# Cross-attention in a decoder layer: packed score operands laid out together in DRAM, read in fewer and earlier DMAs

## The reference, cut to what matters

```python
def _L0_xattn_ref(x, ctx, pos_map, ctx_pos_map, Wq, Wkv, Wout, bout):   # 32 heads of 16
    q = (x @ Wq).reshape(b, n, N_HEADS, HEAD_DIM)
    k, v = jnp.split(ctx @ Wkv, 2, axis=-1)
    ...
    q = apply_axial_rope(q, pos_map)
    k = apply_axial_rope(k, ctx_pos_map)
    logits = jnp.einsum('bqhd,bkhd->bhqk', q, k) * scale
    w = jax.nn.softmax(logits, axis=-1)
    attn = jnp.einsum('bhqk,bkhd->bqhd', w, v)
    return attn.reshape(b, n, N_HEADS * HEAD_DIM) @ Wout + bout
```

## Time and profile before

| what | us |
|---|---|
| median of 3 runs | 1645.27 (1644.57 to 1647.97) |
| the profiled execution, time | 1629.16 |
| the profiled execution, span | 1627.3 |
| TensorE busy in the span | 1380.9 (85%) |
| VectorE busy | 887.9 (55%) |
| GpSimd busy | 504.4 (31%) |
| ScalarE busy | 472.2 (29%) |
| DMA of the hardware queue, share of 16 engines | 21.3% |

### The profile page before, as it was taken

How to read it: one execution, slowest core, us unless ns; L and a number is a source line. 1 busy time by engine, 2 the same in 40 slices (tenths; PEclk the granted TensorE clock), 3 DMA queues, 4 the chain that set the end, 5 groups by cost and what they waited for, 6 DMA issues and landing times. The chain is left out here.

```text
span 1627.3 us, 24455 instructions
## 1 busy us (share of the span) xinstructions
PE 1380.9 (85%) x8442; PEld 1109.1 (68%) x8442; DVE 887.9 (55%) x1532; ACT 472.2 (29%) x731; POOL 504.4 (31%) x348
## 2 busy tenths in 40 slices
PE   5899999945478888888868569999999999999991
PEld 4677777735356566656645458888887879999990
DVE  5666666655556666766643666655556542222225
ACT  3222222223145455444544221111111113332220
POOL 1122222212533233322300230633315056456234
PEclk9999999977679899899988689999999999999996
DMA  6000000003333333333320950324000033345247
GB/s 278 1 1 0 0 0 0 1 1 124 93 109 112 99 93 112 106 99 100 107 67 2 365 207 20 110 85 146 20 20 33 13 130 136 136 139 184 79 125 250
DMA packets 86268, 150.41 MB, mean 92 GB/s; under 512 B 11696, under 2 KB 54832, under 8 KB 83888
## 3 DMA queue, kind: packets, MB, share of 16 engines
q1 hardware_dynamic: 79920, 114.77, 21.3%
q0 software_dynamic: 6272, 34.61, 6.0%
HBM read 88.25 MB, written 60.56 MB: 91 GB/s over the span
## 5 line engine op out<-in xcount | busy, mean ns | idle before, releaser
L972 DVE TENSOR_REDUCE b_mx<-b_rt 128x4 f32<-128x1024 f32 x128 | 156.5, 1223 | 144.1 <-PE b_rt L797 144.1
L1580 DVE SCALAR_TENSOR_TENSOR residual<-c_yp,c_shared,residual 128x512 f32<-128x512 f32 x176 | 127.4, 745 | 143.0 <-PE c_yp L43 142.9
L1114 ACT ACTIVATE b_pf<-b_rt,b_zero 128x1024 f32<-128x1024 f32 x128 | 142.8, 1116 | 215.3 <-PE b_rt L809 214.7
L797 PE MATMUL b_rt<-b_kT,b_qT 64*128 64x256 f32 x512 | 73.9, 371 | 95.6 <-DMA b_qT<-b_low 89.7
L41 PE MATMUL c_fc<-c_xh,c_w 128*128 128x512 f32 x352 | 137.1, 390 | 0.0
L43 PE MATMUL c_fc<-c_xh,c_w 128*128 128x512 f32 x352 | 137.0, 389 | 0.0
L42 PE MATMUL c_fc<-c_xl,c_w 128*128 128x512 f32 x352 | 137.0, 389 | 0.0
L797 PEld LDWEIGHTS b_rt<-b_kT,b_qT 64*128 64x128 f32 x512 | 44.7, 215 | 132.8 <-issue 63.0
L41 PE MATMUL c_fc<-c_ring,c_xTl 128*128 x312 | 105.2, 337 | 0.0
L43 PE MATMUL c_fc<-c_ring,c_xTh 128*128 x312 | 100.6, 322 | 0.0
L42 PE MATMUL c_fc<-c_ring,c_xTh 128*128 x312 | 100.2, 321 | 0.0
(11 more groups left out here) (288 smaller groups left out, 3510.0 us busy)
## 6 DMA issues: line engine op xcount, KB each, us to landing
c_eraw<-in_c_we POOLq DMA_DIRECT2D x8, 2176.0 KB, 9.7
c_xe<-c_rows_in SPq DMA_DIRECT2D x39, 256.0 KB, 3.1
c_rows_out<-c_ye SPq DMA_DIRECT2D x39, 256.0 KB, 2.1
c_rows_in<-c_xe SPq DMA_DIRECT2D x19, 512.0 KB, 10.2
c_rows_out<-c_xe SPq DMA_DIRECT2D x19, 512.0 KB, 10.1
c_wraw<-in_c_ws SPq DMA_DIRECT2D x11, 768.0 KB, 4.3
b_high<-b_hi SPq DMA_DIRECT2D x32, 256.0 KB, 2.3
b_low<-b_lo SPq DMA_DIRECT2D x32, 256.0 KB, 2.3
```

The costliest lines, as they stand in the source:

```text
L797: last = nc.tensor.matmul(rt[:, e, t * S:(t + 1) * S], qT[r, p, t * P:(t + 1) * P], kT[r, p, :], start=True, stop=True)
L972: nc.vector.tensor_reduce(out=mx[:, :, 2 * p:2 * p + 2].rearrange("p t e -> p e t"), in_=rt[:, 0:2, :].rearrange("p e (t s) -> p e t s", s ...
L1114: nc.scalar.activation(pf[:, s:s + 2, :], rt[:, 2:4, :], ACT.Exp, scale=XD ** -0.5, bias=zero[:, :]).then_inc(e_done, 1)
L1580: nc.vector.scalar_tensor_tensor(out=X[:, t, :], in0=yp[:, (n * 4 + k) % 3, :], scalar=shared[:, t:t + 1], in1=X[:, t, :], op0=ALU.mult, o ...
```

## The change

The two DRAM tables become one, `b_pack`, in which the three terms of a head stand below each other in packed order (48 rows, 50 with the two rows of zeros). `rotated_out` now writes `hi` twice, to terms 0 and 2 for k and to terms 0 and 1 for q, and `lo` once. `chunk` has lost its argument e: one call issues four reads, for each e one of 48 rows into `kT` and one of 50 rows into `qT`. Its step is 4f - 4 instead of 4f - 3 and 4f - 2. The semaphore counts follow: `hi_out` gets 64 a group for each c, `chunk_in` 64 instead of 192.

```diff
-    high_dram = nc.dram_tensor("b_high", (B, 2, XD, HP, 2, S), FP32).ap()
-    low_dram = nc.dram_tensor("b_low", (B, 2, XD + 2, HP, 2, S), FP32).ap()
+    pack_dram = nc.dram_tensor("b_pack", (B, 2, 3 * XD + 2, HP, 2, S), FP32).ap()
...
             def rotated_out(g, n):
                 which, c = n // 2, n % 2
-                for k, (table, split, done, out) in enumerate(((high_dram, hi, rh_done, hi_out), (low_dram, lo, rl_done, lo_out))):
+                for split, done, out, terms in ((hi, rh_done, hi_out, ((0, 2), (0, 1))[which]), (lo, rl_done, lo_out, ((1,), (2,))[which])):
                     sp.wait_ge(done, g * 4 + (n + 1))
                     sp.sem_inc(ready, 1)
-                    sp.dma_start(table[g, which, 0:XD, :, c, :].rearrange("(r i) h s -> (i h) r s", r=2),
-                                 as_f32(split[:, :, c, :])).then_inc(out[c], 16)
-
-            def chunk(g, f, e):
+                    for x in terms:
+                        sp.dma_start(pack_dram[g, which, x * XD:(x + 1) * XD, :, c, :].rearrange("(r i) h s -> (i h) r s", r=2),
+                                     as_f32(split[:, :, c, :])).then_inc(out[c], 16)
+
+            def chunk(g, f):
                 c = f // 2
-                if f % 2 == 0 and e == 0:
-                    sp.wait_ge(hi_out[c], g * 32 + 32)
+                if f % 2 == 0:
+                    sp.wait_ge(hi_out[c], g * 64 + 64)
...
-                at = slice(f % 2 * 8 + e, f % 2 * 8 + 8, 2)
-                for which, packed, terms in ((0, kT, (high_dram, low_dram, high_dram)), (1, qT, (high_dram, high_dram, low_dram))):
-                    for x, term in enumerate(terms):
-                        n = XD + 2 if which == 1 and x == 2 else XD
-                        row = 64 * e + 16 * x
-                        sp.dma_start(as_f32(packed[row:row + n, 4 * f:4 * f + 4, :]), term[g, which, 0:n, at, c, :])\
+                for e in range(2):
+                    at = slice(f % 2 * 8 + e, f % 2 * 8 + 8, 2)
+                    for which, packed, n in ((0, kT, 3 * XD), (1, qT, 3 * XD + 2)):
+                        sp.dma_start(as_f32(packed[64 * e:64 * e + n, 4 * f:4 * f + 4, :]), pack_dram[g, which, 0:n, at, c, :])\
                             .then_inc(chunk_in[f], 16)
...
                     for f in range(4):
-                        for e in range(2):
-                            for d in due(i, live, 4 * f - 3 + e):
-                                chunk(b + d, f, e)
+                        for d in due(i, live, 4 * f - 4):
+                            chunk(b + d, f)
...
-                    pe.wait_ge(chunk_in[p // 4], g * 192 + 192)
+                    pe.wait_ge(chunk_in[p // 4], g * 64 + 64)
...
-                    act.wait_ge(hi_out[n % 2], g * 32 + (16 if n >= 2 else 0))
+                    act.wait_ge(hi_out[n % 2], g * 64 + (32 if n >= 2 else 0))
```

More of the change, by code:

```diff
@@ L724, in _ @@
             for g in range(B):
-                sp.dma_start(low_dram[g, 1, XD:XD + 2, :, :, :].rearrange("r h c s -> (r h c) s"),
+                sp.dma_start(pack_dram[g, 1, 3 * XD:3 * XD + 2, :, :, :].rearrange("r h c s -> (r h c) s"),
                              nm[0:64, :, :].rearrange("p t s -> p (t s)")).then_inc(lo_out[g % 2], 16)
@@ L746, in chunk @@
                     sp.sem_inc(ready, 1)
[L747 to L751, removed]
-                at = slice(f % 2 * 8 + e, f % 2 * 8 + 8, 2)
-                for which, packed, terms in ((0, kT, (high_dram, low_dram, high_dram)), (1, qT, (high_dram, high_dram, low_dram))):
-                    for x, term in enumerate(terms):
-                        n = XD + 2 if which == 1 and x == 2 else XD
-                        row = 64 * e + 16 * x
-                        sp.dma_start(as_f32(packed[row:row + n, 4 * f:4 * f + 4, :]), term[g, which, 0:n, at, c, :])\
+                if fresh(g):
+                    sp.wait_ge(presets, 8)
+                else:
+                    sp.wait_ge(st_mm, (g - 1) * HP + (4 * f + 4))
+                for e in range(2):
+                    at = slice(f % 2 * 8 + e, f % 2 * 8 + 8, 2)
+                    for which, packed, n in ((0, kT, 3 * XD), (1, qT, 3 * XD + 2)):
+                        sp.dma_start(as_f32(packed[64 * e:64 * e + n, 4 * f:4 * f + 4, :]), pack_dram[g, which, 0:n, at, c, :])\
                             .then_inc(chunk_in[f], 16)
```

## The result

| | before | changed | |
|---|---|---|---|
| median, us | 1646.62 | 1543.09 | ratio 0.9364, 95% interval 0.9339 to 0.9389 |
| lowest to highest | 1644.57 to 1651.03 | 1539.67 to 1543.8 | 4 runs each |
| span of the profiled execution | 1627.3 | 1541.6 | |

The changed kernel is 103.5 us faster by the medians. The forecast was 1548 (1533 to 1590). I read its trace by the views used before.

A forecast was written before the change was run, and what follows sets the result against it. TensorE was taken to bound cross-attention, waiting for loads queued behind the maxima and slowed by its clock. 74.8 + 4.7 + 24 + 3 - 7 - 2 = 97.5 us off 1645.3 gave 1548 us, range 1533 to 1590.

The forecast's parts named there:

- Chunk waits: Cross-attention score steps: TensorE's 30 waits for the packed operand load go to nothing, gain 74.8 us.
- Clock in the interior: Six interior groups: without the waits TensorE's granted clock holds the full level, gain 6 x 4.0 = 24 us.
- Clock in groups 0 and 7: First and last group: clock gain taken as 3 us for both, their steps being short and bound by VectorE as well.
- VectorE: Late next in the score steps: costs 1.2 us per interior group, 7 us for six, plus 2 us in groups 0 and 7.
- Start and landing: First chunk of cross-attention: usable 2.4 us after its last read's issue, at 426.2 instead of 430.93, gain 4.7 us.
- below 10 us: Sign in the changed kernel's profile: TensorE's wait for `b_pack` below 10 us in all.
- Writes and uneven reads: Doubled high writes cost taken as 0, upper end 8 us; 50-row reads land in 3 to 4 us, hidden by matmuls.
- Clock stays: Rival: TensorE keeps short pauses and its clock still falls, losing 24 + 3 us; time 1575, chance 0.14.
- it does nothing: Rival: the chunk's real releaser is the exponent matmuls of the group before, so no gain; chance 0.01.
- Maxima become late: Rival: maxima stand behind a chunk and writes in SyncE's queue, 32 pay 1 us each; time 1580, chance 0.09.
- Slower: Rival: the 50-row reads run on one engine, a chunk takes 19 us or more; 1808 at the upper bound, chance 0.04.
- Half the wait stays: Rival: packed reads land late because SyncE issues them later than thought; time 1548 + 40 = 1588, chance 0.06.

The follow-up runs named there:

- early12: Kernel before with the new request order alone (chunk at step 4f - 4), keeping its twelve reads and two tables: 1557.5 us, ratio 0.9459.
- filled: Kernel before with 16 idle 256-column matmuls on TensorE ahead of each chunk wait, in every group but the first: 1638.01 us, ratio 0.9962.
- half_max: Changed kernel with the row maximum taken over the first half of the keys only: 1530.67 us, ratio 0.9302.
- packed_late: Changed kernel with its four packed reads requested at the old places, two at step 4f - 3 and two at 4f - 2: 1609.37 us, ratio 0.9781.
- more_writes: Changed kernel with two more writes of the high part per rotated piece, to a DRAM table nobody reads: 1545.29 us, ratio 0.9390.
- split48: Changed kernel with each 50-row read into qT cut into 48 and 2 rows: 1541.38 us, ratio 0.9374.
- b_again: Kernel before, unchanged, run again for a second trace: 1649.48 us, span 1647.7.
- first two sets: Eight follow-up kernels run on one chip beside the kernel before, whose median there was 1644.19 and 1646.25 us.
- the third: Set of three variants of the changed kernel's start, run on another chip beside the kernel before, whose median there was 1624.12 us.

## Why the prediction was right, and where its terms were off

| term | predicted, us | measured, us | from |
|---|---|---|---|
| interior: chunk waits less VectorE | 52.8 - 7 = 45.8 | 48.3 | idle 53.4 to 5.1 |
| interior: clock | 24 | 25.7 | busy 281.6 to 255.9 |
| groups 0 and 7: idle | 22 - 2 = 20 | 17.5 | idle 14.2 to 5.0 and 24.3 to 16.0 |
| groups 0 and 7: clock | 3 | 12.6 | busy 35.8 to 32.7 and 61.0 to 51.5 |
| start | 4.7 | 1.5 | first step 430.93 to 429.45 |
| sum | 97.5 | 105.7 | 103.5 by the medians |

**Chunk waits** (74.8 us, of them 22.0 in groups 0 and 7): right, all 30 are gone, at the margins worked out. `early12` shows that it is the place in the queue that does most of it.

**Clock in the interior** (24 us): right. 25.7 by the traces, and 27.3 by `filled`, where the order and the reads are those of the kernel before and TensorE's pauses are filled.

**Clock in groups 0 and 7** (3 us): mis-sized, 12.6 measured. I charged these groups little because VectorE binds their short steps. In group 7 that didn't hold: its granted clock went from 0.85 to 0.97 and its work from 61.0 to 51.5 us. The 0.83 in the earlier trace rows called for the same reckoning as in the interior. The idle time there fell by 17.5 us instead of 20, since VectorE's waits in the two groups grew by 4.2 us (from 5.1 to 9.4), where I had taken 2.

**VectorE** (1.2 us a group): too dear. Its waits are 4.4 us in the six interior groups, 0.7 a group, and `half_max` puts the whole at 0.8. The 0.41 us wait at step 5 that I read the earlier trace rows was nearly all of it (0.48 now); the 0.9 that I took for it was the middle of a range whose upper end added the DMA wait that had covered it, and the low parts in front of step 13 cost next to nothing.

**Start and landing** (4.7 us): mis-sized, 1.5 measured, and the one term that was wrong in kind. I took 2.4 us from the last read's issue to its use from interior chunks of twelve reads, and kept it for four. Four reads need 5.3 there, 4.9 in `packed_late`, also above the 3 to 4 us that I had allowed for the uneven read. That took 2.9 us back; the first chunk was issued and the low write landed 0.8 us quicker than counted, so from the low write to the first score step it was 8.9 us instead of 6.9. It is also why the wait for `b_pack` came to 12.2 us; the sign "below 10 us" did not fit my own term either, which leaves 14.9 - 4.7 = 10.2. Beside it, the cross-attention's first DMA goes out 1.4 us later in the changed kernel's trace (375.71 against 374.32 us). This is no cost of the change: over all thirteen traces, whose code up to there is the same, it goes out between 374.3 and 376.7 us. In the interior the same error cost nothing, since the smallest margin was 4.8 us at 2.4 of landing, so some 2 us were left of it. With the old order it takes back most of what the quicker issue gives, as `packed_late` shows.

**Writes and uneven reads** (0): right for the interior, by `more_writes` and `split48`.

**The base.** The 16 us between the first trace and the median were carried over without a reason. `b_again` now gives one, but when the forecast was made it was luck that they stayed. By the spans of the two first traces, 1627.3 and 1541.6, the change would be worth 85.7 us, less than the 97.5 of the sum, because only the second has the pause.

**Luck in the sum.** The forecast lies 5 us from the measured median although the clock of groups 0 and 7 alone was off by 9.6 us; the start (3.2 us) and the idle time of groups 0 and 7 (2.5) erred the other way and took more than half of it back. The mechanism of the two large interior terms, the wait and the clock, was right without such help.

**The rivals.** "Clock stays" and "it does nothing" are refuted by the traces (granted clock 1.00, 30 waits gone). "Maxima become late" is real in `early12` at 7.8 us and absent in the changed kernel. "Slower" is real at 47 rows and absent at 50. "Half the wait stays" did not happen, but `packed_late` is its picture.

Among the experiments, two expectations failed outright, those for `packed_late` and for `filled`; the one for `early12` was missed by 2.5 us. That for `packed_late` kept the landing of twelve reads for four; both took the wait for a stock from which a saving can be subtracted, where it was what the steps left over of a loop. The prediction was spared both, because the change takes the request out of the loop and leaves a margin.

## What to carry to other kernels

Where an engine waits for a load, look first at what stands ahead of its request in the issuing queue. A request behind a hand-over that itself hangs on the waiting engine closes a loop whose length sets most of the period: moving the request ahead of it gave 87 of 103 us, packing the reads alone 35, since fewer and larger reads are issued sooner but land later. The two do not add up, because both remove the same waits. Count the clock as a term of its own, the same matmuls by their busy time at either level, and count it as a gain only where TensorE sets the period: in `filled` the same clock gain was worth 6 us.

## What the runs showed of the hardware that I had not expected

- Four reads of 192 and 200 KB, issued in 1.6 to 1.8 us, are usable 4.9 us (median of `packed_late`) to 5.3 us (first chunk of the changed kernel) after the last issue, and 4.8 with nothing behind them; twelve reads of the same bytes, issued over 5.5 us, 2.3 us after it.
- Cutting the 50-row reads into 47 and 3 rows takes the kernel from 1543 to 1874 us. While TensorE waits, the busy share of the 16 DMA engines is then 0.08, at 28 GB/s, and SyncE itself stands in the issue, 8.6 us for two reads.
- A 50-row read cut into 48 and 2 rows raises the DMA engines' busy share from 0.54 to 0.66 at the same 153 GB/s (`split48`).
- A pause of some 20 us in the feed-forward stage, in which ScalarE waits for something that the profile does not show (8.3 and 7.7 us, marked "remote") and GpSimd for ScalarE's queue (20.8 us instead of 5.8), is in one of two traces of the same kernel (spans 1627.3 and 1647.7 us), in all eight traces of the first two sets and in none on the chip of the third.
